# Attention values with f16 exps as the stationary operand, in a fused attention and mixture-of-experts kernel

## The reference, cut to what matters

```python
scores = einsum('bkgsd,bktd->bkgst', qh, kh) / sqrt(32)
weights = softmax(scores, axis=-1)
out = einsum('bkgst,bktd->bkgsd', weights, vh)
```

## Time and profile before

| | us |
|---|---|
| median of 3 runs | 10138.48 |
| lowest and highest | 10130.77 and 10140.67 |
| the profiled execution | 10143.92 |
| its span | 10142.2 |

### The profile page before, as it was taken

One profiled execution on the slowest core, in us unless ns is written; L12 is line 12 of the kernel. 1 busy time (PEld: TensorE's weight loads), 2 busy tenths in 40 slices (PEclk: granted clock), 3 DMA queues, 4 the chain that ended last, 5 costly groups with the idle time before them and its releaser, 6 DMA issues. The chain is left out here.

```text
span 10142.2 us, 169689 instructions
## 1 busy us (share of the span) xinstructions
PE 9157.7 (90%) x55016; PEld 4601.1 (45%) x55016; DVE 5165.7 (51%) x10907; ACT 3662.6 (36%) x5426; POOL 2411.2 (24%) x3894
## 2 busy tenths in 40 slices
PE   4466689999999999999999999999999999989989
PEld 3322234444444444444444444444444444444457
DVE  7766665555555555555555555555555554222212
ACT  3444444333333333443333433333443343200001
POOL 0022222222222222222222222222222222211111
PEclk8688889999999999999999999999999999999999
DMA  9742134444444444444444444444444444454444
GB/s 364 298 186 75 53 104 127 134 134 130 122 130 123 134 133 131 128 132 119 131 134 130 120 133 121 132 134 131 127 133 119 131 136 128 122 189 145 160 167 165
DMA packets 455196, 1431.29 MB, mean 141 GB/s; under 512 B 90088, under 2 KB 110568, under 8 KB 454128
## 3 DMA queue, kind: packets, MB, share of 16 engines
q1 hardware_dynamic: 360240, 1132.12, 33.2%
q0 software_dynamic: 94016, 287.65, 12.2%
HBM read 1034.41 MB, written 408.21 MB: 142 GB/s over the span
## 5 line engine op out<-in xcount | busy, mean ns | idle before, releaser
L866 PE MATMUL e_y<-e_xt,e_w 128*128 128x512 f16 x14520 | 3518.6, 380 | 0.0
L950 ACT ACTIVATE a_p<-a_sc,a_escale 128x512 f32<-128x512 f32 x2048 | 1406.3, 687 | 3621.2 <-PE a_sc L696 3555.8
L1342 DVE TENSOR_REDUCE a_nmax<-a_mx 128x2 f32<-128x512 f32 x2048 | 1411.6, 689 | 1897.6 <-PE a_mx L713 1882.6
L866 PEld LDWEIGHTS e_y<-e_xt,e_w 128*128 128x128 f16 x14520 | 1372.6, 98 | 1597.5 <-issue 244.4
L887 PE MATMUL e_y<-e_w,e_yt 128*128 128x512 f16 x7480 | 1857.7, 380 | 0.0
L713 PE MATMUL a_mx<-a_ks,a_qs 96*128 96x256 f16 x4096 | 816.9, 282 | 564.0 <-DVE a_nmax L1342 559.2
L682 PE MATMUL a_pv<-a_p,a_v 128*64 128x512 f32 x4096 | 1104.1, 664 | 0.0
L1156 POOL TENSOR_TENSOR a_xres<-a_att,a_xres 128x128 f32<-128x128 f32 x1024 | 469.3, 479 | 2424.9 <-DVE a_att L1367 1886.5
L887 PEld LDWEIGHTS e_y<-e_w,e_yt 128*128 128x128 f16 x7480 | 691.0, 98 | 767.6 <-issue 127.4
L713 PEld LDWEIGHTS a_mx<-a_ks,a_qs 96*128 96x128 f16 x4096 | 370.0, 99 | 1078.2 <-DVE a_nmax L1342 684.9
L696 PE MATMUL a_sc<-a_qs,a_ks 128*128 128x512 f16 x2048 | 794.8, 388 | 58.0 <-ACT a_p L950 45.7
(11 more groups left out here) (231 smaller groups left out, 9787.7 us busy)
## 6 DMA issues: line engine op xcount, KB each, us to landing
e_w<-w_parts SPq DMA_DIRECT2D x935, 512.0 KB, 3.6
f_w<-w_parts SPq DMA_DIRECT2D x153, 512.0 KB, 4.9
w_parts<-w_parts SPq DMA_DIRECT2D x136, 512.0 KB, 4.9
h_w<-w_parts SPq DMA_DIRECT2D x136, 512.0 KB, 6.0
a_x<-in_x SPq DMA_DIRECT2D x64, 1024.0 KB, 5.8
a_xres<-in_x SPq DMA_DIRECT2D x64, 1024.0 KB, 7.8
out<-a_xres SPq DMA_DIRECT2D x64, 1024.0 KB, 8.6
xn_parts<-a_xhl SPq DMA_DIRECT2D x64, 1024.0 KB, 9.6
```

The costliest lines, as they stand in the source:

```text
L866: last = pe.matmul(Y[:, bank, :], w1r[:, t % RING, h, pw, :], xT[:, px, h, :], start=r == 0, stop=r == 3 * HT - 1)
L950: act.activation(PT[:, kv % 2, h, tt, :], SC[:, :], ACT.Exp, scale=escale[:, sp_:sp_ + 1]).then_inc(n["exps"], 1)
L1342: dve.reduce_max(nmax[:, half, kv * G + 2 * gp:kv * G + 2 * gp + 2], MX[:, :, :], AX.X, negate=True).then_inc(n["maxed"], 1)
```

## The change

- `exps` computes each exponential twice, as f32 into PF (two buffers, by q) and rounded to f16 into PH. POOL's new `low_p` subtracts the two into PL, the low part, once per q. `exps(q)` waits for `low_p(q-2)`.
- `values` takes 128x128 blocks of PH and PL as the stationary operand and 34 columns of values as the moving one: 32 of the high part and two of ones, or 32 of the low part. Per unit these are 2 blocks of query rows x 4 heads x 2 key halves x 3 products, 48 matmuls. PV now has query rows on partitions, so `values_out` and `turn_o` go, and `o_out` reads PV. `values` moves from behind `max_score(1)` to behind `turn_max` in the same slot.
- V1 is now f16 and double-buffered, copied by POOL at k=7 from the key parts (`ksrc`), whose low part moves ahead of the high ones; four copies instead of two. `vscale` undoes their scaling in `o_out`.
- MX gets a second bank (OT's), used in turn by q.
- POOL's order gets four `low_p` per slot; the second gather moves behind `low_p(1)`. SP's `load_ctx` no longer waits for the copy of the values.

The core of the diff:

```diff
-        V1 = sb("a_v", [P, 2, KV, 2 * D], F32)
-        PT = sb("a_p", [P, 2, 2, 2, 2 * S], F32)
-        OS = sb("a_o", [P, 2 * S], F32)
+        V1 = sb("a_v", [P, 2, 2, KV, 2 * D + 2], F16)
+        PF = sb("a_p", [P, 2, 2 * S], F32)
+        PH = sb("a_ph", [P, 2, 2, 2, 2 * S], F16)
+        PL = sb("a_pl", [P, 2, 2, 2, 2 * S], F16)
-        MX = ps("a_mx", [P, 2, S], F32)
+        MX = ps("a_mx", [P, 2, 2, S], F32)
-        PV = ps("a_pv", [P, 2 * S], F32)
-        OT = ps("a_ot", [P, 4, P], F32)
+        PV = ps("a_pv", [P, 2, G, 2 * D], F32)
...
             def load_ctx(b, par):
-                at_least(sp, n["v_made"], (b - 1) * 2)
+                at_least(sp, n["k_low"], b - 1)
                 settle(sp, sp_passed)
-                at_least(sp, n["k_low"], b - 1)
...
             def values(i, k, par):
...
-                pe.wait_ge(n["exps"], b * 32 + (4 * kv + 4))
+                vp = (1 - par) if k >= 6 else par
+                pe.wait_ge(n["p_low"], b * 32 + (4 * kv + 4))
                 pe.wait_ge(n["v_made"], b * 2 + 2)
-                at_least(pe, n["o_there"], b * 8 + kv)
-                for tt in range(2):
-                    for h in range(2):
-                        last = pe.matmul(PV[2 * D * h:2 * D * (h + 1), :], V1[:, tt, kv, :],
-                                         PT[:, kv % 2, h, tt, :], start=tt == 0, stop=tt == 1)
+                at_least(pe, n["o_done"], b * 8 + kv)
+                for c in range(2):
+                    for g in range(G):
+                        cols = slice((g % 2) * S + c * P, (g % 2) * S + (c + 1) * P)
+                        for tt in range(2):
+                            pe.matmul(PV[:, c, g, 0:D + 2], PH[:, kv % 2, g // 2, tt, cols],
+                                      V1[:, vp, tt, kv, 0:D + 2], start=tt == 0, stop=False)
+                            pe.matmul(PV[:, c, g, 0:D], PH[:, kv % 2, g // 2, tt, cols],
+                                      V1[:, vp, tt, kv, D + 2:2 * D + 2], start=False, stop=False)
+                            last = pe.matmul(PV[:, c, g, 0:D + 2], PL[:, kv % 2, g // 2, tt, cols],
+                                             V1[:, vp, tt, kv, 0:D + 2], start=False, stop=tt == 1)
...
-                at_least(pe, n["maxed"], b * 32 + (4 * kv + q))
+                at_least(pe, n["maxed"], b * 32 + (4 * kv + q - 1))
...
-                    turn_o(i, k)
...
-                    values(i, k, par)
...
                     turn_max(i, k)
+                    values(i, k, par)
...
             def exps(i, k, par, q):
...
-                act.activation(PT[:, kv % 2, h, tt, :], SC[:, :], ACT.Exp,
+                at_least(act, n["p_low"], b * 32 + (4 * kv + q - 1))
+                act.activation(PF[:, q % 2, :], SC[:, :], ACT.Exp, scale=escale[:, sp_:sp_ + 1])
+                act.activation(PH[:, kv % 2, h, tt, :], SC[:, :], ACT.Exp,
                                scale=escale[:, sp_:sp_ + 1]).then_inc(n["exps"], 1)
...
             def copy_values(b, par):
-                wait_par(pool, ctx_got, b, par)
-                at_least(pool, n["pv"], b * 8)
+                pool.wait_ge(n["k_low"], b + 1)
+                settle(pool, passed)
+                at_least(pool, n["pv"], (b - 1) * 8)
                 settle(pool, passed)
                 for c in range(2):
-                    pool.tensor_copy(V1[:, c, :, 0:D], cin[:, par, c, :].rearrange("p (v d) -> p v d", d=D))\
+                    pool.tensor_copy(V1[:, par, c, :, 0:D + 2], ksrc[:, c, :, 2 * D:3 * D + 2])
+                    pool.tensor_copy(V1[:, par, c, :, D + 2:2 * D + 2], ksrc[:, c, :, 0:D])\
                         .then_inc(n["v_made"], 1)
+
+            def low_p(i, k, q):
+                b, kv = scu(i, k)
+                if on(b):
+                    pool.wait_ge(n["exps"], b * 32 + (4 * kv + q + 1))
+                    pool.tensor_tensor(PL[:, kv % 2, q // 2, q % 2, :], PF[:, q % 2, :],
+                                       PH[:, kv % 2, q // 2, q % 2, :], ALU.subtract).then_inc(n["p_low"], 1)
...
                 for k in range(8):
+                    low_p(i, k, 0)
                     if k == 0 and on(i):
                         pool.wait_ge(n["ctx_max"], i + 1)
                         at_least(pool, n["ctx_chain"], i * 4)
...
                     if k == 2 and soon:
                         gather(m1, par, 0)
-                        gather(m1, par, 1)
...
+                    low_p(i, k, 1)
+                    if k == 2 and soon:
+                        gather(m1, par, 1)
...
                     attended(i, k, par)
+                    low_p(i, k, 2)
...
-                    if k == 5 and on(i - 1):
-                        copy_values(i - 1, 1 - par)
...
+                    low_p(i, k, 3)
                     if k == 7 and on(i - 4):
                         scatter(i - 4)
+                    if k == 7 and on(i):
+                        copy_values(i, par)
                     if k == 7 and now:
                         add_rows(m, 1 - par, 2)
```

More of the change, by code:

```diff
@@ L464, in fuse @@
                      "q_turned", "q_there", "k_turned", "k_there", "max_scores", "maxed",
-                     "max_turned", "max_high", "max_low", "scores", "exps", "pv", "o_there", "o_turned",
+                     "max_turned", "max_high", "max_low", "scores", "exps", "p_low", "pv", "vscaled",
                      "o_recip", "o_done", "x1_done",
@@ L668, in _ @@
         def _(pe):
-            pe.wait_ge(filled, 3)
+            pe.wait_ge(filled, 2)
             pe.wait_ge(rows_cleared, 3)
@@ L709, in max_score @@
                     pe.wait_ge(n["k_there"], b * 2 + 2)
-                at_least(pe, n["maxed"], b * 32 + (4 * kv + q))
+                at_least(pe, n["maxed"], b * 32 + (4 * kv + q - 1))
                 for g2 in range(2):
                     g = 2 * gp + g2
-                    last = pe.matmul(MX[:, g2, :], QS[0:96, kv, g * S + half * P:g * S + half * P + P],
+                    last = pe.matmul(MX[:, q % 2, g2, :], QS[0:96, kv, g * S + half * P:g * S + half * P + P],
                                      KS[0:96, mp, kv, :], start=True, stop=True)
@@ L789, in turn_rows @@
                 last.then_inc(turned, 1)
[L791 to L801, removed]
             def turn_max(i, k):
@@ L936, in _ @@
         def _(act):
-            act.wait_ge(filled, 3)
+            act.wait_ge(filled, 2)
             def exps(i, k, par, q):
@@ L990, in high_k @@
                     at_least(act, n["k_turned"], b * 2)
+                    at_least(act, n["v_made"], b * 2)
                 for c in range(2):
-                    act.activation(ksrc[:, c, :, s * D:(s + 1) * D],
+                    act.activation(ksrc[:, c, :, (s + 1) * D:(s + 2) * D],
                                    cin[:, par, c, :].rearrange("p (v d) -> p v d", d=D),
@@ L1089, in iteration @@
                     k_out(i, k, par)
-                    values_out(i, k)
                     experts(i, 8 * k + 5, par, fused)
@@ L1154, in attended @@
                     for c in range(2):
-                        to = xres[:, bp, c, u * P:(u + 1) * P].rearrange("p (h g d) -> p g h d", h=2, g=2)
-                        pool.tensor_tensor(to, att[:, u % 2, 2 * c:2 * c + 2, :, :], to, ALU.add)\
+                        to = xres[:, bp, c, u * P:(u + 1) * P]
+                        pool.tensor_tensor(to, att[:, u % 2, c, :, :].rearrange("p g d -> p (g d)"), to, ALU.add)\
                             .then_inc(n["x1_done"], 1)
@@ L1341, in max_out @@
                         at_least(dve, n["max_turned"], b * 4 + (kv // 2) - 3)
-                    dve.reduce_max(nmax[:, half, kv * G + 2 * gp:kv * G + 2 * gp + 2], MX[:, :, :],
+                    dve.reduce_max(nmax[:, half, kv * G + 2 * gp:kv * G + 2 * gp + 2], MX[:, q % 2, :, :],
                                    AX.X, negate=True).then_inc(n["maxed"], 1)
@@ L1357, in q_out, with o_out @@
                     last.then_inc(n["q_there"], 1)
-            def o_out(i, k):
+            def o_out(i, k, par):
                 b, u = otu(i, k)
                 if on(b):
-                    dve.wait_ge(n["o_turned"], b * 8 + (u + 1))
+                    vp = (1 - par) if k >= 7 else par
+                    dve.wait_ge(n["pv"], b * 8 + (u + 1))
                     at_least(dve, n["x1_done"], b * 16 + 2 * (u - 1))
-                    ot = OT[:, :, :].rearrange("p q (v d) -> p q v d", v=2)
-                    dve.reciprocal(orec[:, u % 2, :, :], ot[:, :, :, D]).then_inc(n["o_recip"], 1)
+                    dve.reciprocal(orec[:, u % 2, :, :], PV[:, :, :, D]).then_inc(n["o_recip"], 1)
                     dve.wait_ge(n["o_recip"], b * 8 + (u + 1))
-                    dve.tensor_tensor(att[:, u % 2, :, :, :], ot[:, :, :, 0:D],
-                                      orec[:, u % 2, :, :].unsqueeze(3).to_broadcast([P, 4, 2, D]),
-                                      ALU.mult).then_inc(n["o_done"], 1)
```

(11 more changed lines are left out.)

17 lines of the change are left out of this document (6 added, 11 removed).

## The result

The changed kernel takes 10466.83 us (median of 4 runs, 10462.44 to 10470.57), the kernel before beside it 10139.58 (4 runs, 10130.77 to 10145.11): a ratio of 1.0323, with a 95% interval of 1.0306 to 1.0341. It is slower by 3.2%; the forecast was 10,510, 3.7%, and the range 10,230 to 10,800. The profiled execution took 10468.8 us, its span is 10467.1, 324.9 more than before's.

What follows compares the result with a forecast made beforehand. PE was taken to bound steps 13 to 63, no engine being full before. Expert pairs +286, units after step 63 -25, early steps +110: +371 on 10138.5 gives 10,510 us, range 10,230 to 10,800.

Steps and rivals of the forecast that it cites:

- where the stall forms: Slot 0 to 1: `low_p(1)` stands behind both POOL code changes, `exps(3)` waits for it, PE's `score(0)` for that; 18.2 us later.
- The values product: PE's 48 new matmuls per unit at 25.4 ns, 1.22 us, replacing 2.31 us: a gain of 1.1 us per slot.
- Rival C: The 48 matmuls are paced by their loads at 56 ns instead of 25.4: +560, 11,070 us; chance 7%.
- `low_p` and the exps: POOL's 32 subtractions per step at 1.2 us, 38 us; ACT's second activation of 0.687 us each, 22 us more per step.
- The size of the stall: POOL stands still 9.9 us before the all-reduce and 8.8 after it; PE idles some 21 us.
- rival B: Gain and stall cancel, POOL's two waits being some 7 us per step shorter: 10,150 us; chance 4%.
- first kind of step: Expert steps of 132.3 us, alternating with those of 145.1; there `score(0)` of slot 1 comes 18.2 us later.
- The clock: Half clock after a PE stall, 2.2 us lost after the present 8.48 us one: plus 2.0 us per pair of expert steps.
- The early steps: Steps 2 to 12: half of a some 20 us passage from scatter to `score(0)`, +10 us per step, +110.
- the lower bound of this term: Early steps at -5 us each: the values product gains everywhere and nothing more happens.
- A: PE is relieved and the wait never forms: -600, 9,540 us; chance 11%.
- D: The forecast with its sizes off: stall ±150, early steps -165 or +110, matmul price up to +190; 10,230 to 10,800; 78%.

Runs made afterwards that it cites:

- experiment 1: Changed kernel with POOL's all-reduce replaced by two small DMAs through HBM and a DVE reduction: 9520.09 us, ratio 0.9417 to the kernel before.
- experiment 4: Changed kernel with all `low_p` calls on DVE instead of POOL, the all-reduce left on POOL: 9706.61 us, ratio 0.9601 to the kernel before.
- experiment 5: Changed kernel with a second all-reduce per step, of a constant column, at slot 4, result unused: 10864.46 us, ratio 1.0746 to the kernel before.
- experiment 8: Changed kernel without the all-reduce, values copies at slot 6, freed bank given to the scores instead of the maxima: 9699.37 us, ratio 0.9579.
- experiment 9: Changed kernel without the all-reduce, values copies at slot 6, three PF buffers instead of two: 9440.99 us, ratio 0.9323 to the kernel before.

## Why the prediction was right

**What bounds it, and where the stall forms.** Right. PE bounds the expert steps, `low_p(1)` stands behind both changes of POOL's code, and the chain `low_p`, exps, score holds PE once per step (1211.7 us of waits, up to 18.2 each). Experiments 1 and 4 remove the wait in two ways, and 5 pays 429 us for a second all-reduce. By kind of step the forecast's terms come to +11.8 and -0.6 us; steps 16 to 55 of the traces have +10.0 (132.2 to 142.2) and -0.9 (144.1 to 143.2).

**The values product.** Right: 25.2 ns per matmul against 25.4 assumed, and 9.0 us less work per step where 8 times 1.1 was the term. Rival C (56 ns) is out. So are the up to 3.9 us that the prediction worked out from the 81 ns at 128 columns of the Trainium skill (TensorE: Matmul & The Clock Gate, Back-to-back issue gap): the 48 took 1.21 us. 34 moving columns cost no more here than the 8 of the earlier trace rows, with a full load each. The reason given, that streaming hides behind the load, was the wrong way round for the 56 ns: a full load fits into 25.2 ns, and from 128 to 512 columns (56 and 216 ns) each column costs 0.42 ns, so that 128 columns make 53 of the 56 by themselves.

**`low_p` and the exps.** 1.18 us against 1.2, and 0.688 and 0.682 us against 0.687.

**The size of the stall.** A little too large. The forecast had 9.9 and 8.8 us from the earlier trace rows. The second held (553.5 us in 63 steps, 8.8). The first fell to 7.3: in the earlier trace rows it begins behind a scatter-add, now behind the copies and `low_p(0)`, and in experiment 5, with no DMA issue just ahead of it, it is 6.0. So some 2.6 us per step of the 9.9 could lie beside other work. That is rival B's mechanism, in part; it was priced at 7 us. PE's idle time at the late score, forecast at some 21 us in the first kind of step, is 15.9 there on average. In the account of a step, the forecast's terms leave -8.8 for the work and +1.0 for the clock out of +5.6 in all, so +13.4 for the gaps: 10.7 were measured, 2.7 less.

**The clock.** The term was undersized: 2.0 us per pair, taken from one stall of 8.48 us, where 2.9 per step, 5.8 per pair, were lost. Both kinds of step now have a long stall, and in the step shown PE ran for 5.7 us after it came back at half the clock (3104.86 to 3110.6).

The two errors have opposite signs, -2.7 and +1.9 us per step, and the work is 0.2 us less than forecast: -1.0 us per step in steps 16 to 55. Over steps 13 to 62 it is -0.7, the difference between 280 and 244. So the total is nearer than its terms, and that part is luck.

**The early steps.** The size was right (97 us against 110), the reason was not, so this term came out by luck. I halved a stall of 20 us; the account of early steps 3 to 11 shows something else:

```
us per early step                    step    work at full clock    gaps    lost at half clock
before                               84.0         38.0             40.0           6.0
before, without the all-reduce       78.1         37.9             34.6           5.7
after                                92.7         26.5             45.6          20.5
after, without the all-reduce        79.8         26.9             32.4          20.5
```

The gaps grew by 5.6 us only. The work shrank by 11.5, but 14.5 more were lost to the lower clock, granted for 77 of 92.7 us where it was 31 of 84.0. Even without the all-reduce the change makes an early step 1.6 us longer. So the lower bound of this term, that the values gain everywhere, rested on a full clock that this stage does not get. Which part of the new arrangement brings the clock down there wasn't isolated; experiments 1, 8 and 9 all show it (0.61, 0.65 and 0.61 in seven early steps), so it isn't the all-reduce.

**The rivals.** A's price, 9,540, is what experiment 1 gives (9,520) once the all-reduce is gone, though more of it than forecast is the second MX bank: the forecast gave that 1.5 us per pair besides the 8.48 us stall, and it is worth 284 us. B falls: the second wait did not shrink, and PE still stalls for 15.9 us per step before scores. B's own 10,150 lies below the range too, so A, B and C leave out 22% and not 18; and the bounds of the range are a choice, as the terms of D at their ends, added up, give 10,195 and 10,960. By the Trainium skill (GPSIMD Engine Reference, Instruction dispatch) a first call after loading would take some 6 us; the trace agrees for the change to the all-reduce where no DMA stands ahead of it (6.0), and the way back costs as much again (6.8 to 8.8).

## What to carry to other kernels

Before you put work on the path into an in-order queue, look for what in that queue stands still without a reason in the profile: here 16 to 19 us per step that cost 131 us while little that was urgent stood behind them, and 919 once PE's operands were. Remove such a stop, or move the urgent work to another queue, before the change is judged. And when a change makes the bounding engine's work shorter, price the waits and the clock that it meets next: 11.5 us less work per early step gave nothing back.

## What had not been expected of the hardware

POOL's subtractions slow some of DVE's small operations. Two lines of the changed kernel, and the same two with `low_p` on DVE (experiment 4):

```profile
L1480 DVE SCALAR_TENSOR_TENSOR e_th<-e_th 64x512 f32<-64x512 f32 x55 | 68.4, 1243 | 1.9
...
L1272 DVE TENSOR_TENSOR a_eq<-a_logit,a_m 128x16 f32<-128x16 f32 x128 | 65.3, 510 | 4.4
```

```profile
L1476 DVE SCALAR_TENSOR_TENSOR e_th<-e_th 64x512 f32<-64x512 f32 x55 | 37.6, 683 | 1.9
...
L1261 DVE TENSOR_TENSOR a_eq<-a_logit,a_m 128x16 f32<-128x16 f32 x128 | 25.5, 199 | 4.4
```

1243 ns against 683 and 510 against 199, for the same operations; the reductions of the maxima, which read a PSUM bank, stay at 688 and 686. The means hide two groups of calls. Below are the shortest, median and longest call (ns) of L1480 in the changed kernel, and of L1477, the operation just before it, of the same kind and shape but with one input in a PSUM bank:

```profile
L1480 DVE SCALAR_TENSOR_TENSOR e_th<-e_th x55: 682/1428/2744, 1521.2 to 9113.7; 64x512 f32<-64x512 f32 x55
L1477 DVE SCALAR_TENSOR_TENSOR e_th<-e_th,e_y x55: 666/669/679, 1520.5 to 9113.0; 64x512 f32<-64x512 f32 x55
```

Of the 55 calls of L1480, 27 run beside no `low_p` and take 682 to 684 ns. The other 28 overlap one, take 1783 ns on average, and each ends 553 to 556 ns after that `low_p` does. L1272 has 67 calls of 175 ns and 61 of 878 in the same way. L1477 overlaps a `low_p` in 27 of its calls and takes 668 ns in them, 670 in the others. The Trainium skill (SBUF — State Buffer, SBUF: two separate sides) has DVE and GpSimd share a pair of ports, which a DVE operation with two SBUF inputs and a GpSimd operation hold in turn for a whole instruction. The trace agrees: the operations with two SBUF inputs come through only at the end of a `low_p`, and those that read PSUM are not held. The ports themselves are not seen in a trace, and no run tried them alone. DVE had the room, so it cost no time that I could find.

The other surprise is the clock in the early stage, above: 0.81 became 0.59 with the shorter matmuls, and it is 0.56 to 0.65 in every version that has them.
